# A two-layer Perceiver block: the state-space convolution as products of transforms, FiLM by token rows, norms by tile, and a new order in the top-32 attention

## The chip, the cores and the metric

The kernel runs on one NeuronCore of one Trainium2 chip, in fp32. The time is device microseconds of one execution. PE is the matrix engine (PEld its weight loads), DVE the vector engine, ACT the scalar engine, POOL GpSimd, SP the engine that issues most DMAs.

## The reference, cut to what matters

x is 8 batches of 64 tokens of 512 values, so 512 token rows, four tiles of 128. Six blocks follow one another, each `x = x + block(norm(x))`: cross attention to a context of 1601 rows, causal attention, experts, the block of this case, causal attention with rotary positions, experts with capacity.

```python
scores = where(mask, (x@Wq)(ctx@Wk)/sqrt(32)); keep top 32 per row; softmax; mean over 4 heads
c_t = (mean_weights @ (ctx@Wv)) * text_mask
x = layernorm(x_text, g_norm_in, b_norm_in)
scale_in, shift_in = split(c_t @ W_film_in + b_film_in)
x = x * (1 + gate * scale_in) + gate * shift_in
y = irfft(rfft(x, 2L) * rfft(K, 2L))[:L] + x * D_skip      # causal convolution, L = 64, per channel
y = y * (1 + gate * scale_out) + gate * shift_out
xt = x_text + y
xt = xt + gelu(layernorm(xt, g_ffn, b_ffn) @ W1 + b1) @ W2 + b2
out = layernorm(xt, g_norm_out, b_norm_out)
```

## The kernel before

Each block is one or two stages. A stage runs five engine programs side by side; at its end all engines meet in a barrier. Within a stage semaphores set the order, and the calls of each engine are written out by hand. Matmuls are fp32; each is two records in the trace.

**Context stage (d2), `xattn1_context`.** It loops over 8 batches. On PE `keys(b)` projects the context, `score(b)` makes two sets (r = 0, 1) of 128x1601 scores, `average(b)` averages the heads' weights into a transposed mean, `blend(b)` multiplies it with the context and turns the result. On DVE `pick(b, r)` takes the top 32 in four rounds of `max` and `match_replace`; after the second round of `pick(b, 0)` it runs `invert(b - 1)`, which waits for ACT's `exponentials(b - 1, 1)`. POOL subtracts, which gives the sparse weights. ACT runs `exponentials(b, r)`, copies keys, scores and means out of PSUM, and makes `share` from `invert`'s result; `average` waits for it. Before, ACT takes `put_keys(b + 2)` ahead of `exponentials(b, 1)` and PE takes `keys` and `score` ahead of `average`.

**FiLM and MLP stage (d3), `film_and_mlp`.** Channels lie on partitions. After the value product (L3165) the normed input is transposed (L3171); FiLM factors are made for four channel chunks (L3182) and copied out by ACT. The 64-tap convolution is shared: DVE takes chunks 0 and 1, a multiply-add per tap (L3055), POOL chunk 2 from taps scaled by ACT, PE chunk 3 with diagonal matrices (L3197). The result is transposed back (L3203), normed over all four tiles at once, transposed (L3208), scaled by DVE (L3088), and goes through W1 (L3216) and W2 (L3225, the last quarter of W2 lying in `w_out_film`). Then DVE adds, norms and adds x (L3098 to L3106).

**Next attention (e).** Its weights are loaded at its start (L1147, L1265). It norms x (`Norm.on_vector`, L138 to L146), and PE transposes (L1305) once all four tiles are normed; so do the other causal attention (b) and both expert stages (c, f).

## Time and profile before

| | us |
|---|---|
| median of 3 runs | 2467.47 (2466.85 to 2469.83) |
| the profiled execution | 2466.18 |
| span of its trace | 2464.5 |
| context stage | 1419 to 1741 |
| FiLM and MLP stage | 1741 to 2015 |
| next attention | 2017 to 2108 |

Starts are counted from the beginning of the span. An engine's row gives what it did, for how long, and in brackets how long it stood idle before and what ended that.

### The profile page before, as it was taken

Reading aid. Unit: us, or ns where it says so; the run is one execution under the profiler, and the core shown is the slowest. Engines: PE = TensorE matmul, PEld = TensorE weight load, DVE = VectorE, ACT = ScalarE, POOL = GpSimd, SP = SyncE. Lnnn points to the kernel's source line nnn. Section 1 sums busy time; section 2 is a strip of 40 time slices with the busy share of each in tenths; the row PEclk is TensorE's granted clock in tenths of the full one; section 3 lists DMA queues with packets and bytes.
Section 4 is the critical chain, followed back from the end, with each engine's and each line's share of the span. In section 5 each row is a group of like instructions: output and inputs, shape, how many; then the busy total and the mean of one; then the engine's idle time right before and its main releaser. Section 6 shows DMA issues by size and latency. Waiting matters only on the chain. (4 is left out here: it accounts for less than half of the span.)

```text
span 2464.5 us, 27034 instructions
## 1 busy us (share of the span) xinstructions
PE 2212.8 (90%) x10178; PEld 1333.9 (54%) x10178; DVE 1062.0 (43%) x2105; ACT 739.5 (30%) x1480; POOL 464.7 (19%) x535
## 2 busy tenths in 40 slices
PE   7989999999999986899999978887994968799999
PEld 3545555555555533444444435555452435699998
DVE  5465654655655124100000169778595034422120
ACT  2344444444544212211111143443280111111111
POOL 0000000000000010489986112112080000000010
PEclk9999999999999998899999986786896988899999
DMA  6102122122121321888887372431410010556662
GB/s 204 39 21 78 49 69 77 43 73 79 36 78 48 109 77 40 317 312 310 315 311 294 128 248 80 160 120 55 172 46 0 0 70 3 227 219 260 226 234 74
DMA packets 131282, 326.68 MB, mean 133 GB/s; under 512 B 39841, under 2 KB 89153, under 8 KB 111570
## 3 DMA queue, kind: packets, MB, share of 16 engines
q1 hardware_dynamic: 99440, 297.20, 33.6%
q10 hardware_dynamic: 29010, 19.16, 2.5%
q0 software_dynamic: 2704, 8.59, 1.0%
q8 instruction: 83, 1.36, 0.2%
q14 instruction: 45, 0.37, 0.0%
HBM read 302.89 MB, written 20.91 MB: 131 GB/s over the span
## 5 line engine op out<-in xcount | busy, mean ns | idle before, releaser
L874 PE MATMUL a_mix<-a_xn,a_probs_T 128*128 128x384 f32 (+1 forms) x832 | 313.1, 493 | 15.1 <-issue 10.2
L803 PE MATMUL a_sc<-a_wk_centred,a_ctx_T 128*128 128x512 f32 x624 | 288.3, 599 | 4.9 <-DVE a_wk_centred L552 2.6
L874 PEld LDWEIGHTS a_mix<-a_xn,a_probs_T 128*128 128x128 f32 (+1 forms) x832 | 145.8, 191 | 120.6 <-issue 73.0
L1830 PE MATMUL c_gate_up<-c_w_wide,c_h_rows 128*128 128x512 f32 x480 | 210.9, 592 | 0.0
L803 PEld LDWEIGHTS a_sc<-a_wk_centred,a_ctx_T 128*128 128x128 f32 x624 | 117.7, 192 | 129.4 <-issue 105.0
L1734 DVE TENSOR_TENSOR c_hidden<-c_silu,c_gate_up 128x512 f32<-128x512 f32 x38 | 26.1, 688 | 365.5 <-PE c_gate_up L1830 354.1
L1830 PEld LDWEIGHTS c_gate_up<-c_w_wide,c_h_rows 128*128 128x128 f32 x480 | 90.2, 190 | 108.0 <-issue 108.0
L2290 PE MATMUL f_ring<-f_picked_T,f_w 128*128 128x160 f32 x1024 | 143.5, 300 | 0.0
L2305 PE MATMUL f_ring<-f_hidden,f_w 128*128 128x160 f32 x1024 | 141.4, 300 | 0.4 <-ACT f_hidden L2179 0.4
L2290 PEld LDWEIGHTS f_ring<-f_picked_T,f_w 128*128 128x128 f32 x1024 | 139.9, 190 | 0.2
L2305 PEld LDWEIGHTS f_ring<-f_hidden,f_w 128*128 128x128 f32 x1024 | 139.3, 190 | 0.9 <-ACT f_hidden L2179 0.6
L1873 PE MATMUL c_y<-c_w_down,c_hidden_T 128*128 128x512 f32 x304 | 136.6, 593 | 0.0
L462 DVE SCALAR_TENSOR_TENSOR a_keys<-a_k_bias,a_std,a_sc 128x512 f32<-128x512 f32 (+1 forms) x104 | 77.1, 741 | 129.0 <-PE a_sc L803 129.0
L421 POOL TENSOR_SCALAR a_mask<-a_mask 128x896 bf16<-128x896 uint8 x8 | 7.5, 941 | 625.3 <-DVE a_top L491 607.1
L616 ACT ACTIVATE a_sq<-a_keys 128x512 f32<-128x512 f32 (+1 forms) x104 | 65.6, 630 | 196.2 <-DVE a_keys L462 196.2
L2841 PE MATMUL d_mean<-d_share,d_scores 128*128 128x64 f32 (+1 forms) x416 | 87.5, 414 | 21.8 <-ACT d_share L2747 9.1
L491 DVE CUSTOM_DVE_ANT_0 a_probs<-a_sc,a_mask 128x896 f32<-128x896 f32 x64 | 67.3, 1089 | 82.6 <-PE a_sc L834 82.6
L2841 PEld LDWEIGHTS d_mean<-d_share,d_scores 128*128 128x128 f32 (+1 forms) x416 | 86.0, 325 | 23.2 <-issue 12.9
L2647 POOL TENSOR_TENSOR d_scores<-d_scores,d_left 128x1601 f32<-128x1601 f32 x15 | 51.0, 3399 | 231.1 <-ACTq L2740 231.1
L3055 DVE SCALAR_TENSOR_TENSOR d_conv<-d_xin,kern,d_conv 128x504 f32<-128x504 f32 (+62 forms) x126 | 88.6, 703 | 4.6
L2663 DVE MAX8 d_best<-d_left 128x8 f32<-128x1601 f32 x48 | 87.6, 1826 | 1.4
L2667 DVE MATCH_REPLACE8 d_left<-d_best,d_left 128x1601 f32<-128x1601 f32 x48 | 86.9, 1811 | 0.0
(525 smaller groups left out, 3508.3 us busy)
## 6 DMA issues: line engine op xcount, KB each, us to landing
c_w_wide<-in_L_ffn_W SPq DMA_DIRECT2D x68, 1024.0 KB, 6.9
f_w<-in_L_ffn_W SPq DMA_DIRECT2D x32, 2048.0 KB, 8.5
c_w_down<-in_L_ffn_W SPq DMA_DIRECT2D x34, 1024.0 KB, 7.2
a_ctx_T<-in_ctx_T SPq DMA_DIRECT2D x48, 384.0 KB, 3.5
a_xn<-in_ctx SPq DMA_DIRECT2D x24, 768.0 KB, 7.1
d_context_T<-in_ctx_T SPq DMA_DIRECT2D x24, 768.0 KB, 10.7
d_context<-in_ctx SPq DMA_DIRECT2D x8, 2304.0 KB
mixed_context<-a_mixed_T ACTq DMA_DIRECT2D x84, 64.0 KB, 1.8
```

Source lines behind the costliest of these rows:

```text
L462: dve.scalar_tensor_tensor(out=keys[0:m, n % 4, :], in0=k_bias[0:m, :], scalar=std[0:m, t:t + 1], in1=key_bank(b, t)[0:m, :], op0=ALU.mult ...
L491: dve.tensor_tensor_reduce(out=probs[:, n % 2 * 2 + h, :].rearrange("p (c n) -> p c n", c=2), in0=sc[h][:, :, 0:BANK], in1=mask[:].rearran ...
L803: last = pe.matmul(key_bank(b, t), ctx_T[:, n % AHEAD, k, cols], wk_centred[:, k, :], start=(k == 0), stop=(k == KC - 1))
L874: ins = pe.matmul(mix[:, 0:DC], probs_T[0:m, t, p * P:(p + 1) * P], xn[0:m, b % 2, t, :], start=(t == 0), stop=(t == CT - 1))
L1830: last = pe.matmul(gate_up[2 * (u % 2) + part][:], h[:, k, :], w_wide[:, i % WIDE_RING, k, :], start=(k == 0), stop=(k == KD - 1))
L1873: last = pe.matmul(y[t % 2][:], hidden_T[:, u % 2, k, :], w_down[:, i % DOWN_RING, k, :], start=(c == 0 and k == 0), stop=(c == 1 and k == ...
L2290: last = pe.matmul(ring[use % 3][:, (m - lo) * CAP:(m - lo + 1) * CAP], w1[:, i % CHUNKS, k, at:at + P], picked_T[:, e % 2, k, :], start=( ...
L2305: last = pe.matmul(ring[use % 3][:, (m - lo) * CAP:(m - lo + 1) * CAP], w2[:, i % CHUNKS, k, at:at + P], hidden[:, k, :], start=(k == 0), ...
L2663: own.did(dve.max(eight, src))
L2667: ins = dve.match_replace(left[:, r, :], eight, src, MASKED)
L2841: last = pe.matmul(mean[t // 8][0:m, t % 8, :], scores[:, b % KEEP, r, t * P:t * P + m], share[:, r, :], start=(r == 0), stop=(r == 1))
L3055: own.did(dve.scalar_tensor_tensor(out=out[:, :, l:SEQ], in0=src[:, :, 0:SEQ - l], scalar=g.kern[:, k, l:l + 1], in1=out[:, :, l:SEQ], op0 ...
```

## The change

The convolution becomes products with constant matrices of cosines and sines (`waves`, a new input): with tokens on partitions, `transform(t)` takes two batches of a tile to 128 spectrum rows each, DVE multiplies by the kernel's spectrum (`multiply`), `transform_back(t)` sums two products back to 64 tokens per batch. FiLM factors come out by token rows and DVE applies them from PSUM. The norm before W1 runs tile by tile; ACT scales three turned tiles and DVE the last. The end of the block runs tile by tile and makes the next attention's norm as well; that attention's weights are loaded into W1's room once W1 is used up. In attention b and expert stages c and f, PE starts to transpose with the first normed tile (the hunk of b and e is shown; e has no norm left to wait for). In the context stage the order of ACT, PE and the loads changes. A stage `h` is put around d3 and e.

Of film_and_mlp the new lines are shown; what they replace stands above.

```diff
         def _(pe):
-            pe.wait_ge(norm.normed, NT)
             for t in range(NT):
+                if not normed:
+                    pe.wait_ge(norm.normed, t + 1)
                 for k in range(KD):
                     last = pe.transpose(ring[t][:, k, :], g.hn[:, t, k * P:(k + 1) * P], g.ident[:])
...
             load_turned(3)
+            load_turned(4)
             for b in range(2, NB):
                 load_context(b)
-                if b + 2 < NB:
-                    load_turned(b + 2)
+                if b + 3 < NB:
+                    load_turned(b + 3)
             early.load(sp, d)
...
             act.wait_ge(stack_ready, 2)
+            exponentials(0, 0)
+            put_keys(2)
             for b in range(NB):
-                exponentials(b, 0)
-                if b >= 1:
-                    put_mix(b - 1)
-                if b + 2 < NB:
+                exponentials(b, 1)
+                if 1 <= b and b + 2 < NB:
                     put_keys(b + 2)
-                exponentials(b, 1)
-                if b + 2 < NB:
-                    put_scores(b + 2)
                 if b < NB - 1:
                     put_shares(b)
                 put_mean(b)
+                if b < NB - 1:
+                    exponentials(b + 1, 0)
+                    put_mix(b)
+                if b + 2 < NB:
+                    put_scores(b + 2)
             put_mix(NB - 1)
...
             score(1)
+            keys(2)
             pe.wait_ge(stack_ready, 2)
             for b in range(NB):
-                if b + 2 < NB:
-                    keys(b + 2)
-                    score(b + 2)
                 average(b)
                 blend(b)
+                if b + 2 < NB:
+                    score(b + 2)
+                if b + 3 < NB:
+                    keys(b + 3)
...
+class Ahead:
+    def __init__(self, s):
+        self.room = s.sb("room", [P, KD * 2048])
+        self.w = self.room[:, 0:KD * 10 * P].rearrange("p (k n) -> p k n", k=KD)
+        self.wo = self.room[:, KD * 10 * P:KD * 14 * P].rearrange("p (k n) -> p k n", k=KD)
+        self.wv = self.room[:, KD * 14 * P:KD * 14 * P + KD * 32].rearrange("p (k n) -> p k n", k=KD)
+        self.qk_in, self.v_in, self.o_in = s.sem("qk_in"), s.sem("v_in"), s.sem("o_in")
+    def load(self, sp, d):
+        for h in (slice(0, KD // 2), slice(KD // 2, KD)):
+            sp.dma_start(self.w[:, h, :], d["L1_attn_qk"][:, h, :]).then_inc(self.qk_in, 16)
+        sp.dma_start(self.wv, d["L1_attn_wv"]).then_inc(self.v_in, 16)
+        sp.dma_start(self.wo, d["L1_attn_wo"]).then_inc(self.o_in, 16)
...
+            sp.wait_ge(ring_full, R_WIDE + FC)
+            ahead.load(sp, d)
...
+            norm.on_vector(dve, g.hn, xin)
+            gate = vecs["mod_gate"][:, 0:1]
+            def gated(t):
+                own.did(dve.tensor_scalar(t[:, 0:D], t[:, 0:D], gate, 1.0, ALU.mult, ALU.add))
+                own.did(dve.tensor_scalar(t[:, D:2 * D], t[:, D:2 * D], gate, None, ALU.mult))
+            gated(early_long["b_film_in"])
+            def each(out, left, right, op):
+                for t in range(NT):
+                    own.did(dve.tensor_tensor(out[:, t, :], left[:, t, :], right, op))
+                own.wait()
+            each(xin, xin, early_long["g_norm_in"][:], ALU.mult)
+            each(xin, xin, early_long["b_norm_in"][:], ALU.add)
+            each(rest, xin, early_long["b_film_in"][:, 0:D], ALU.mult)
+            each(rest, rest, early_long["b_film_in"][:, D:2 * D], ALU.add)
+            def modulate(t):
+                u = R_IN + 2 * t
+                dve.wait_ge(ring_full, u + 1)
+                own.did(dve.tensor_tensor(xin[:, t, :], xin[:, t, :], ring[u % 4][:], ALU.mult))
+                own.wait()
+                dve.tensor_tensor(rest[:, t, :], rest[:, t, :], xin[:, t, :], ALU.add).then_inc(film_out, 1)
+                dve.wait_ge(film_out, 2 * t + 1)
+                dve.wait_ge(ring_full, u + 2)
+                own.did(dve.tensor_tensor(xin[:, t, :], rest[:, t, :], ring[(u + 1) % 4][:], ALU.add))
+                own.wait()
+                dve.sem_inc(film_out, 1)
+                dve.sem_inc(modulated, 1)
+            def multiply(b):
+                dve.wait_ge(spectrum_full, b + 1)
+                dve.tensor_tensor(hidden[:, b, :], y[b % 4][:], kern_re[:], ALU.mult).then_inc(spectrum_out, 1)
+                dve.tensor_tensor(hidden[:, NB + b, :], y[b % 4][:], kern_im[:], ALU.mult).then_inc(spectrum_out, 1)
+            def finish(t):
+                u = R_OUT + 2 * t
+                dve.wait_ge(ring_full, u + 1)
+                dve.tensor_tensor(rest[:, t, :], b_film_out[:, 0:D], ring[u % 4][:], ALU.add
+                                  ).then_inc(film_out, 1)
+                dve.wait_ge(film_out, 2 * NT + 2 * t + 1)
+                dve.wait_ge(signal_full, t + 1)
+                own.did(dve.tensor_tensor(rest[:, t, :], rest[:, t, :], y[t][:], ALU.mult))
+                own.wait()
+                own.did(dve.tensor_tensor(rest[:, t, :], rest[:, t, :], xt[:, t, :], ALU.add))
+                own.wait()
+                dve.wait_ge(ring_full, u + 2)
+                own.did(dve.tensor_tensor(xt[:, t, :], rest[:, t, :], ring[(u + 1) % 4][:], ALU.add))
+                own.wait()
+                dve.sem_inc(film_out, 1)
+            def measure(i, t, src):
+                own.did(dve.bn_stats(end_stats[:, i, t, :], src))
+                own.wait()
+                dve.bn_aggr(end_mv[:, i, t, :], end_stats[:, i, t, :]).then_inc(end_measured, 1)
+            def normalize(i, t, src, dst, done=None):
+                dve.wait_ge(end_rooted, ROOTS.index((i, t)) + 1)
+                own.did(dve.reciprocal(end_rstd[:, i, t:t + 1], end_rstd[:, i, t:t + 1]))
+                own.wait()
+                ins = dve.tensor_scalar(dst, src, end_mv[:, i, t, 0:1], end_rstd[:, i, t:t + 1], ALU.subtract, ALU.mult)
+                if done is not None:
+                    ins.then_inc(done, 1)
+                else:
+                    own.did(ins)
+                    own.wait()
+            def add_hidden(t):
+                dve.wait_ge(y_full, t + 1)
+                own.did(dve.tensor_tensor(xt[:, t, :], xt[:, t, :], y[t][:], ALU.add))
+                own.wait()
+                measure(1, t, xt[:, t, :])
+            def end_tile(t):
+                normalize(1, t, xt[:, t, :], xt[:, t, :])
+                own.did(dve.tensor_tensor(xt[:, t, :], xt[:, t, :], long["g_norm_out"][:], ALU.mult))
+                own.wait()
+                own.did(dve.tensor_tensor(g.x[:, t, :], g.x[:, t, :], xt[:, t, :], ALU.add))
+                own.wait()
+                measure(2, t, g.x[:, t, :])
             for t in range(NT):
+                modulate(t)
+                if t == 0:
+                    dve.wait_ge(kern_out, 3)
                 else:
+                    multiply(2 * t - 2)
+                    multiply(2 * t - 1)
+            dve.wait_ge(b_out_in, 16)
+            gated(b_film_out)
             own.wait()
+            each(xt, g.hn, b_film_out[:, D:2 * D], ALU.add)
+            multiply(2 * NT - 2)
+            multiply(2 * NT - 1)
             for t in range(NT):
+                finish(t)
+                measure(0, t, xt[:, t, :])
+                if t:
+                    normalize(0, t - 1, xt[:, t - 1, :], g.hn[:, t - 1, :], mlp_normed)
+            normalize(0, NT - 1, xt[:, NT - 1, :], g.hn[:, NT - 1, :], mlp_normed)
             dve.wait_ge(long_in, 16 * len(long))
             for t in range(NT):
                 own.did(dve.tensor_tensor(xt[:, t, :], xt[:, t, :], long["b2"][:], ALU.add))
+            dve.wait_ge(turned_full, NT)
+            for k in range(KD):
+                last = dve.tensor_scalar(turned[:, k, (NT - 1) * P:NT * P], y[NT - 1][:, k * P:(k + 1) * P],
+                                         vecs["g_ffn"][:, k:k + 1], vecs["b_ffn"][:, k:k + 1], ALU.mult, ALU.add)
+            last.then_inc(scaled_by_dve, 1)
             for t in range(NT):
                 own.did(dve.tensor_tensor(g.x[:, t, :], g.x[:, t, :], long["b_norm_out"][:], ALU.add))
             own.wait()
+            for i in range(NT + 2):
+                if i < NT:
+                    add_hidden(i)
+                if 0 <= i - 1 < NT:
+                    end_tile(i - 1)
+                if 0 <= i - 2 < NT:
+                    normalize(2, i - 2, g.x[:, i - 2, :], g.hn[:, i - 2, :])
...
+            act.dma_start(waves[:], d["waves"]).then_inc(waves_in, 16)
+            act.dma_start(b_film_out[:], rows(d["L1_xattn_b_film_out"])).then_inc(b_out_in, 16)
+            act.wait_ge(kern_full, 1)
+            act.activation(kern_T[0:SEQ, :], y[0][0:SEQ, :], ACT.Copy).then_inc(kern_out, 1)
             norm.on_scalar(act, g.eps[:])
+            act.wait_ge(v_in, early.v_count)
             for m in range(KD):
                 act.wait_ge(ring_full, m + 1)
+                act.activation(value_T[:, m, :], ring[m % 4][:], ACT.Copy, scale=vecs["mod_gate"][:, 0:1]).then_inc(value_out, 1)
+                if m == 1:
+                    for i, t in enumerate((kern_re, kern_im)):
+                        act.wait_ge(kern_full, 2 + i)
+                        act.activation(t[:], y[1 + i][:], ACT.Copy).then_inc(kern_out, 1)
+            def root(n):
+                i, t = ROOTS[n]
+                act.wait_ge(end_measured, n + 1)
+                act.activation(end_rstd[:, i, t:t + 1], end_mv[:, i, t, 1:2], ACT.Sqrt, bias=g.eps[:]).then_inc(end_rooted, 1)
+            def scale(t):
+                act.wait_ge(turned_full, t + 1)
+                for k in range(KD):
+                    last = act.activation(turned[:, k, t * P:(t + 1) * P], y[t][:, k * P:(k + 1) * P], ACT.Identity,
+                                          bias=vecs["b_ffn"][:, k:k + 1], scale=vecs["g_ffn"][:, k:k + 1])
+                last.then_inc(scaled_by_act, 1)
+            root(0)
+            root(1)
+            root(2)
+            scale(0)
+            scale(1)
+            root(3)
+            scale(2)
             for m in range(FC):
                 u = R_WIDE + m
                 act.wait_ge(ring_full, u + 1)
                 act.activation(hidden[:, m, :], ring[u % 4][:], ACT.Gelu,
+                               bias=vecs["b1"][:, m:m + 1]).then_inc(wide_out, 1)
+            for n in range(NT, len(ROOTS)):
+                root(n)
...
+            for k in range(KD):
+                last = pe.transpose(y[0][0:SEQ, k * P:(k + 1) * P], g.kern[:, k, :], g.ident[:])
+            last.then_inc(kern_full, 1)
+            def values(m):
                 for k in range(KC):
                     last = pe.matmul(ring[m % 4][:], w_v[:, k, m * P:(m + 1) * P], c_T[:, k, :], start=(k == 0),
                                      stop=(k == KC - 1))
                 last.then_inc(ring_full, 1)
+            pe.wait_ge(w_v_in, 16)
+            pe.wait_ge(masked, KC)
+            values(0)
+            values(1)
+            pe.wait_ge(waves_in, 16)
+            pe.wait_ge(kern_out, 1)
+            for i, w in enumerate((taps_re, taps_im)):
+                pe.matmul(y[1 + i][:], w[0:SEQ, :], kern_T[0:SEQ, :], start=True, stop=True).then_inc(kern_full, 1)
+            values(2)
+            values(3)
+            pe.wait_ge(value_out, KD)
             pe.wait_ge(w_film_in, 32)
+            def film(t, outer):
                 w = w_out_film if outer else w_in_film
                 for j in range(2):
+                    n = (2 * NT if outer else 0) + 2 * t + j
+                    u = R_IN + n
+                    if n >= 4:
+                        pe.wait_ge(film_out, n - 3)
                     for i in range(KD):
+                        last = pe.matmul(ring[u % 4][:], value_T[:, i, t * P:(t + 1) * P], w[:, i, j * D:(j + 1) * D],
                                          start=(i == 0), stop=(i == KD - 1))
                     last.then_inc(ring_full, 1)
+            def transform(t):
+                pe.wait_ge(modulated, t + 1)
+                if t == 0:
+                    pe.wait_ge(kern_out, 3)
+                for b in (2 * t, 2 * t + 1):
+                    if b >= 4:
+                        pe.wait_ge(spectrum_out, 2 * (b - 4) + 2)
+                    half = slice(b % 2 * SEQ, (b % 2 + 1) * SEQ)
+                    pe.matmul(y[b % 4][:], forward[half, :], xin[half, t, :], start=True, stop=True
+                              ).then_inc(spectrum_full, 1)
+            def transform_back(t):
+                pe.wait_ge(spectrum_out, max(4 * t + 4, 2 * (t + 4) + 2))
+                for i, w in enumerate((back_re, back_im)):
+                    for h in range(2):
+                        last = pe.matmul(y[t][h * SEQ:(h + 1) * SEQ, :], w, hidden[:, i * NB + 2 * t + h, :],
+                                         start=(i == 0), stop=(i == 1), skip_group_check=True)
+                last.then_inc(signal_full, 1)
+            film(0, False)
+            film(1, False)
+            transform(0)
+            film(2, False)
+            transform(1)
+            film(3, False)
+            transform(2)
+            film(0, True)
+            transform(3)
+            film(1, True)
+            transform_back(0)
+            transform_back(1)
+            film(2, True)
+            transform_back(2)
+            transform_back(3)
+            film(3, True)
             for t in range(NT):
+                pe.wait_ge(mlp_normed, t + 1)
                 for k in range(KD):
                     last = pe.transpose(y[t][:, k * P:(k + 1) * P], g.hn[:, t, k * P:(k + 1) * P], g.ident[:])
                 last.then_inc(turned_full, 1)
+            pe.wait_ge(scaled_by_act, NT - 1)
+            pe.wait_ge(scaled_by_dve, 1)
...
+                    if q == 3:
+                        last.then_inc(y_full, 1)
...
+                with Stage(nc, "h") as s2:
+                    ahead = Ahead(s2)
+                    film_and_mlp(g, early, ahead)
+                    causal_attention(g, "e", "L1_attn_qk", 1, True, "L1_attn_wv", 32, "L1_attn_wo", None,
+                                     1.0 / float(np.sqrt(32.0)), ahead)
```

## Rows read from the trace of the kernel before

**Rows 1.** The page: busy tenths of PE in 40 slices, and two costly groups (busy us, mean ns).

```profile
PE   7989999999999986899999978887994968799999
...
L2663 DVE MAX8 d_best<-d_left 128x8 f32<-128x1601 f32 x48 | 87.6, 1826 | 1.4
L2667 DVE MATCH_REPLACE8 d_left<-d_best,d_left 128x1601 f32<-128x1601 f32 x48 | 86.9, 1811 | 0.0
```

**Rows 2.** Windows: stretch, span, busy us (x count) by engine, granted PE clock, DMA share, GB/s.

```profile
1488.00:1492.00 4.00, 4.00 (x21) 4.00 (x21) 3.93 (x5) 0.32 (x1) 0.00 (x0) 0.50 0.00 0
1756.00:1784.00 28.00, 28.00 (x72) 12.82 (x71) 23.22 (x42) 5.44 (x7) 3.13 (x2) 1.00 0.41 159
```

**Rows 3.** Timeline of PE, FiLM and MLP stage: start us, duration us, [idle before].

```profile
1743.09 11.97 PE L3165 MATMUL d_ring<-d_c_T,d_w_v 128*128 128x512 f32 x24 [3.43 <-DVE d_c_T L3021]
...
1756.64 27.63 PE L3182 MATMUL d_ring<-d_value_T,d_w_in_film 128*128 128x512 f32 x64
...
1870.70 3.67 PE L3203 MATMUL d_y<-ident,d_conv 128*128 128x128 f32 x16 [26.50 <-DVE d_conv L3066]
...
1887.05 58.02 PE L3216 MATMUL d_ring<-d_xin,d_w_wide 128*128 128x512 f32 x128 [2.80 <-DVE d_xin L3088]
...
1986.10 13.90 PE L3225 MATMUL d_y<-d_w_out_film,d_hidden 128*128 128x512 f32 x32
```

**Rows 4.** Timeline of DVE, the same stage.

```profile
1826.79 36.85 DVE L3055 SCALAR_TENSOR_TENSOR d_conv<-d_xin,kern,d_conv 128x504 f32<-128x504 f32 x63
...
1864.40 0.69 DVE L3043 TENSOR_TENSOR d_conv<-d_conv,d_hidden 128x512 f32<-128x512 f32 x1
...
1881.80 5.19 DVE L3088 TENSOR_SCALAR d_xin<-d_y,d_v_g_ffn,d_v_b_ffn 128x128 f32<-128x128 f32 x16 [1.28 <-PE d_y L3208]
1886.90 2.49 DVE L3094 TENSOR_TENSOR d_xt<-d_xt,d_r_b 128x512 f32<-128x512 f32 x4
```

**Rows 5.** Waits of DVE, context stage: us in total, times, longest.

```profile
DVE d_total L2678 <- ACTq L2740: 30.2, 5, 7.3
```

**Rows 6.** Timeline of DVE, context stage: `invert` of the first and seventh batch.

```profile
1482.59 0.17 DVE L2678 RECIPROCAL d_total<-d_total 128x2 f32<-128x2 f32 x1
...
1693.53 0.17 DVE L2678 RECIPROCAL d_total<-d_total 128x2 f32<-128x2 f32 x1
```

**Rows 7.** Timeline of PE, context stage: one round and two `score` calls.

```profile
1452.91 1.13 PE L2818 MATMUL d_ks<-d_k_T,d_q_diag 64*128 64x512 f32 x4
...
1484.55 10.95 PE L2841 MATMUL d_mean<-d_share,d_scores 128*128 128x64 f32 x52 [1.49 <-ACT d_share L2747]
1495.42 7.09 PE L2857 MATMUL d_mix<-d_context,d_mean_T 128*64 128x384 f32 x26
1503.09 0.88 PE L2864 MATMUL d_turned<-d_stack,d_mixed 128*128 128x64 f32 x6 [0.58 <-ACT d_mixed L2763]
1503.81 8.56 PE L2807 MATMUL d_ks<-d_context_T,d_wk 128*128 128x512 f32 x24
...
1517.62 2.08 PE L2818 MATMUL d_ks<-d_k_T,d_q_diag 64*128 64x512 f32 x4 [2.90 <-ACT d_scores L2717]
```

**Rows 8.** Timeline of ACT, context stage.

```profile
1456.91 1.32 ACT L2717 ACTIVATE d_scores<-d_ks 128x512 f32<-128x512 f32 x4 [0.45 <-PE d_ks L2822]
...
1483.89 0.60 ACT L2747 ACTIVATE d_share<-d_quarter,d_total 128x64 f32<-128x64 f32 x2
```

**Rows 9.** Timeline of DVE, end of the MLP and start of the next stage.

```profile
2012.97 2.50 DVE L3106 TENSOR_TENSOR x<-x,hn 128x512 f32<-128x512 f32 x4
2016.78 2.47 DVE L138 BATCH_NORM_STATS2 e_norm_stats<-x 128x6 f32<-128x512 f32 x4 [1.32 <-PEq L90]
...
2020.25 1.91 DVE L146 TENSOR_SCALAR hn<-x,e_norm_mv,e_norm_rstd 128x512 f32<-128x512 f32 x4
```

**Rows 10.** Timeline of PE at that start.

```profile
2022.22 2.19 PE L1305 MATMUL e_ring<-ident,hn 128*128 128x128 f32 x9 [22.22 <-DVE hn L146]
```

**Rows 11.** DMA issues, 1740 to 1770 us: KB each, us to landing.

```profile
d_w_out_film<-in_L_xattn_W_film_out SPq DMA_DIRECT2D x1, 2048.0 KB, 12.4
```

289 lines of the change are left out of this document (73 added, 216 removed).

## The prediction

> **What bounds the kernel now.** I read the page first. PE is nine tenths busy in most slices, with dips in the second half [rows 1], so time is to be had where PE waits, and those places lie in the two stages that the change rewrites. The waits, the timelines of PE and DVE and a table of windows then say what bounds each place.
>
> *Context stage.* Between the reciprocals of the first and the seventh batch lie 210.9 us, 35.2 a round [rows 6]. DVE's only wait there is 30.2 us in five pieces, for the exponentials of r = 1 [rows 5]: `invert` stands in the middle of `pick`, and ACT, its releaser, first copies keys that PE is still making. Without that wait a batch would take (210.9 - 30.2) / 6 = 30.1 us of DVE, 3.8 for each of its eight pairs of `max` and `match_replace` (1.83 and 1.81 busy) [rows 1].
>
> *FiLM and convolution.* PE makes 64 film records from 1756.64 on in 27.5 us, 0.43 each at the full clock, and as many again for the second matrix, to 1811.6 [rows 2, 3]. Then DVE sets the pace: its second chunk alone is 36.9 us of taps [rows 4], and PE stands idle for 26.5 us before it can turn the result [rows 3]. W1 starts at 1887.05.
>
> *After the MLP.* The last W2 record ends at 2000.0 [rows 3], DVE adds and norms until 2015.5 (2012.97 + 2.50), then come two barriers, and one more norm of four tiles; PE turns its first tile at 2022.22 after 22.2 us of idleness [rows 9, 10].
>
> **The change part by part.** The sum is made against the profiled execution, 2466.18 us; the median of the runs is 1.3 above it, and the forecast for the median is moved by as much. The smallest change that this kernel's measurement can tell is about 0.2%, 5 us.
>
> *1. Context order.* ACT now takes `exponentials(b, 1)` first, so DVE's wait of 30.2 goes. What is late next is the scores. `score(b + 2)` moves behind `average(b)` and `blend(b)`, and `average` needs `share`, which needs `invert`, 7.6 us into `pick(b + 1, 0)`. The loop from one start of a pick to the next is then: two pairs 7.6, the reciprocal 0.2 [rows 6], `share` 0.6 [rows 8]; `average` 10.9 (1484.55 to 1495.42); `blend`, the copy and the turn 8.4 (to 1503.81) [rows 7]; `score` and its copies, 1452.91 to 1458.23 less the last copy, 5.0 [rows 7, 8]. That is 32.7, above DVE's 30.1. PE's own work in it is 10.9 + 8.4 + 8.6 (`keys`) + 4.1 = 32.0, so it is nearly full. The reason for a little less: `average` ran at half clock [rows 2], 0.21 a record, behind a wait of 1.5; now only some 0.7 us of idleness come ahead of it. At the pace of the turning records, 0.88 / 6 = 0.147, it would take 7.6. I take 32.3: 6 x (35.2 - 32.3) = 17 gained. Bounds: DVE's pace of 30.1 gives 30; `score` with two of four pieces at half clock, 2.08 for 1.13 as at 1517.62 [rows 7], adds 2 a round and leaves 3. POOL's subtraction runs beside DVE's pairs as before; the load of `keys(b + 3)` is issued a round ahead, behind one `blend`.
>
> *2. Convolution.* Removed: 126 taps of DVE, 63 of POOL, 128 diagonal records, two sets of transposes. PE's chain, from the same start (values end at 1755.0 [rows 3]): two products for the kernel's spectrum, four records, 1.7; the last value copy, by the copy ahead of the turn (0.58 for 384 columns [rows 7]), 0.7; so films start at 1757.4. Films: 16 x 8 records x 0.43 = 55.0. `transform`: four tiles, each two products on different row halves like `score`'s four records in 1.13 [rows 7], 4.3 together. `transform_back`: 8 records a tile on column halves like `blend`. There 26 records of 384 columns took 7.09, 0.27 each, partly at half clock; 1.9 a tile at full clock, 7.6 together. Were the halves not to overlap, it would be 8 x 0.43 = 3.4 a tile and 1.7 for a `transform`: 6 and 2.5 more. Film work ends at 1757.4 + 55.0 + 4.3 + 7.6 = 1824.3.
>
> DVE stays under that. Its 16 row operations before the first tile cost 0.62 each (L3094's 2.49 / 4) [rows 4], and end near 1760, when the first film bank (1757.4 + 3.4) is full; four banks are a cover of 6.9 us, after which each us late is one of PE. A tile then needs 3 operations of 0.73 to modulate (0.69 and a step) and 4 to multiply, 5 us against PE's 6.9; at the end 4 more and the norm, beside 6.9 of film again.
>
> Behind the film work: PE turns tiles 0 and 1 (3.67 / 4 = 0.92 each [rows 3]). ACT's order is `scale(0)`, `scale(1)`, and only then the last root; each `scale` costs four operations, by DVE's 5.19 / 16 = 0.32 some 1.3. So the root comes at 1824.3 + 0.9 + 2.6 = 1827.8, with it and DVE's two small steps the last tile is normed at 1828.8. Queued on DVE ahead of its own scaling are the four additions of b2, 2.5; they hide the transpose of tile 3. Scaling 1.3 and a crossing: W1 starts at 1832.8, 54.3 earlier. Bounds: 57 with transposes at full clock and a shorter end, 45.5 with no overlap of halves. Loads: `w_out_film` landed 12.4 us after an issue half a microsecond into the stage, near 1753.8, as the last of 4 MB [rows 11]. The 0.77 MB that ACT now issues beside them cost 2.3 at that rate: 1756.1, before 1757.4. Were `waves` to land only then, PE would stand 6 us before the kernel's products.
>
> One rule speaks against many small products between the films. PE takes `blend` on 64 columns at 1495.42, before `average`'s last record on 128 ends [rows 7], so I see no gap. 
>
> *4. End of the block.* Tiles of W2 come 3.4 us apart, the last at 2000.0 on the old axis. DVE per tile, with a step of 0.11 after each dependent operation: add 0.73, measure 0.85; two factors and an addition 3.0 with the second measure; the next norm 0.7. That is 5.3, above 3.4, so DVE sets the end: first two tiles to 1997.7, then 5.3, 5.3 and 4.4, 2012.7. The pieces are from 2.47 / 4 and 1.91 / 4 [rows 9] and rows 4. One barrier, half of the 1.3 between 2015.47 and 2016.78 [rows 9]: PE turns its first tile at 2013.4 instead of 2022.2, 8.8 gained. The next attention's weights, loaded beside W2, have 55 us for 3.7 MB; without that they would now be waited for. Bounds: 6, if every root's crossing shows, to 11, if the steps vanish.
>
> *5. Stage `h`* adds barriers at the end of attention e, two times 0.65: 1.3 lost.
>
> *6. Transposes with the first tile* in b, c and f: three tiles of 1.91 / 4 = 0.48 [rows 9], 1.4 each, 4.3 gained; at 0.92 a tile PE stays behind DVE, so all of it passes on. If the work behind waits for loads it is 1.
>
> Sum: -17 - 54.3 - 8.8 + 1.3 - 4.3 = -83. 2466.2 - 83 = 2383, and 2384 for the median.
>
> **The rivals.**
> - *The new order gains nothing.* PE's 32.0 of work a round leaves no slack; a little more half clock in `score` makes it the old 35. For it: `score` at 1517.62 at half clock behind an idle 2.9. Against: `keys` and `score` now follow `blend` without a pause. 17 less 3 lost: 2398.
> - *DVE's pace.* `average` runs at full clock, a round is 30.1: 13 more, 2371. Against it: the `average` of rows 2 stood at 0.50.
> - *Stalls in the film stage*, from halves that don't overlap or `waves` late: 8 to 14 more, 2392 to 2398.
> - *Slower.* PE, denser now, is held at 1.2 GHz. Film work is 72 us at full clock and the MLP 113; each would double. It decides from 83 us of such work on: the film stage alone gives 2456, both 2569. Against it: the granted clock was 1.00 in a stretch without a gap [rows 2].
>
> **How the numbers follow.** Forecast 0.58, its own range 2374 to 2394; order without gain 0.14; DVE's pace 0.12; stalls 0.13; slower 0.02; within 0.2% 0.01. All bounds at once give 102 and 54 less, 2366 and 2414. From 2368 to 2404 the range takes in all cases but the ends of two and the last two, at most 2 in 10. Faster 0.97, same 0.01, slower 0.02.
>
> **What would show it.** Reciprocals of `invert` 32 to 33 us apart, and DVE's wait now for scores; W1 starting 92 us after the value product's stage begins, with PE without a gap over 1 us from the first film to the last; the last normed tile waiting for a root behind `scale(1)`; some 13 us from the last W2 record to the first transpose of the next attention. Wrong would make it: PE idle between films (loads, or DVE behind), clock under 1.0 in the film stage, rounds of 35, or weights of the next attention waited for.

## The result and the profile after

| | before | after |
|---|---|---|
| median | 2467.16 us (2465.91 to 2469.83, 4 runs) | 2385.72 us (2384.64 to 2387.93, 4 runs) |
| span of the trace | 2464.5 | 2384.3 |
| mean granted clock of PE | 0.931 | 0.947 |

The ratio is 0.967, with an interval of 0.9653 to 0.9686. The change takes 81.4 us, where 83 were forecast. The stages show how well that sum was made (each from its start to the next one's; us). They are read from the two profiled executions, and add up to 80.2 less:

| stretch | before | after | difference | forecast |
|---|---|---|---|---|
| first stage (a) | 884.2 | 884.9 | +0.7 | 0 |
| attention b | 94.9 | 95.6 | +0.7 | -1.4 |
| experts c | 440.2 | 440.0 | -0.2 | -1.4 |
| context stage | 321.7 | 295.1 | -26.6 | -17 |
| FiLM stage, to the first W1 record | 146.0 | 94.1 | -51.9 | -54.3 |
| W1 and W2 | 113.0 | 112.9 | -0.1 | 0 |
| last W2 record to the next attention's first transpose | 22.2 | 14.1 | -8.2 | -8.8 |
| from there to stage f | 86.9 | 91.8 | +4.9 | +1.3 |
| experts f | 355.4 | 355.9 | +0.5 | -1.4 |

So the total is right partly by luck: the context stage gave 9.6 more than forecast, and the other stretches 12.4 less together.

**Context stage.** Timeline of DVE, the reciprocal of `invert` in the first and the seventh batch; it answers to [rows 6]:

```profile
1483.70 0.17 DVE L2692 RECIPROCAL d_total<-d_total 128x2 f32<-128x2 f32 x1
...
1668.96 0.17 DVE L2692 RECIPROCAL d_total<-d_total 128x2 f32<-128x2 f32 x1
```

Six rounds take 185.3, 30.9 each, and not 32.3; they alternate between 31.5 to 31.8 and 30.1. The waits of DVE in this stage, which answer to [rows 5], have no wait for an exponential any more:

```profile
DVE d_best L2677 <- ACT d_scores L2731: 24.5, 4, 20.1
```

Of these 24.5 us, 20.1 are the first scores, at the start. The other 4.4, three waits of about 1.5, are what makes every second round longer than 30.1: there DVE waits for scores, as the prediction had it for all rounds. Timeline of PE, the first three calls of `average` (52 records) and one of `blend` (26), which answer to [rows 7]:

```profile
1484.58 10.91 PE L2857 MATMUL d_mean<-d_share,d_scores 128*128 128x64 f32 x52 [17.25 <-ACT d_share L2761]
...
1516.82 5.81 PE L2857 MATMUL d_mean<-d_share,d_scores 128*128 128x64 f32 x52 [0.79 <-ACT d_share L2761]
1522.56 4.73 PE L2873 MATMUL d_mix<-d_context,d_mean_T 128*64 128x384 f32 x26
...
1546.47 10.94 PE L2857 MATMUL d_mean<-d_share,d_scores 128*128 128x64 f32 x52 [4.41 <-ACT d_share L2761]
```

The same 52 records take 10.9 or 5.8 us in turn: behind an idle stretch of 0.79 they are quick, behind one of 4.41 slow. The windows, of the first and the second `average`, say at which clock; the column behind the last busy time is the granted one:

```profile
1488.00:1492.00 4.00, 4.00 (x21) 4.00 (x21) 3.97 (x4) 0.32 (x1) 0.00 (x0) 0.50 0.00 0
1517.00:1521.00 4.00, 4.00 (x38) 4.00 (x38) 3.93 (x4) 0.36 (x1) 0.00 (x0) 1.00 0.88 291
```

**FiLM stage.** Timeline of PE from the stage's start to W1, which answers to [rows 3]:

```profile
1717.66 8.08 PE L3213 MATMUL d_ring<-d_c_T,d_w_v 128*128 128x512 f32 x12 [1.44 <-DVE d_c_T L3041]
1725.68 1.98 PE L3224 MATMUL d_y<-d_kern_T,d_waves 64*128 64x512 f32 x4
1727.59 5.42 PE L3213 MATMUL d_ring<-d_c_T,d_w_v 128*128 128x512 f32 x12
1733.78 14.00 PE L3239 MATMUL d_ring<-d_w_in_film,d_value_T 128*128 128x512 f32 x32 [0.78 <-ACT d_value_T L3172]
1747.71 1.13 PE L3251 MATMUL d_y<-d_xin,d_waves 64*128 64x512 f32 x4
1748.77 7.13 PE L3239 MATMUL d_ring<-d_w_in_film,d_value_T 128*128 128x512 f32 x16
...
1780.21 3.65 PE L3259 MATMUL d_y<-d_hidden,d_waves 128*64 128x512 f32 x16
...
1794.44 7.13 PE L3239 MATMUL d_ring<-d_w_out_film,d_value_T 128*128 128x512 f32 x16
1801.41 1.04 PE L3282 MATMUL d_y<-ident,hn 128*128 128x128 f32 x8
1804.11 0.66 PE L3282 MATMUL d_y<-ident,hn 128*128 128x128 f32 x4 [1.66 <-DVE hn L3104]
1805.96 1.11 PE L3282 MATMUL d_y<-ident,hn 128*128 128x128 f32 x4 [1.20 <-DVE hn L3104]
1809.70 57.93 PE L3294 MATMUL d_ring<-d_xin,h_room 128*128 128x512 f32 x128 [2.62 <-issue]
```

From the first film to 1801.5 PE has no gap: 67.7 us, forecast 66.9. A transform takes its 1.13, two of `transform_back` 3.65. The stage itself starts at 1715.62 with the kernel's transposes, which are not shown. Behind the films come three short idle stretches up to W1. ACT and DVE in those, from their timelines:

```profile
1802.05 2.90 ACT L3186 ACTIVATE d_xin<-d_y,d_v_b_ffn,d_v_g_ffn 128x128 f32<-128x128 f32 x8 [5.62 <-PE d_y L3282]
1804.81 0.33 ACT L3181 ACTIVATE d_end_rstd<-d_end_mv,eps 128x1 f32<-128x1 f32 x1
```

```profile
1805.16 0.16 DVE L3102 RECIPROCAL d_end_rstd<-d_end_rstd 128x1 f32<-128x1 f32 x1 [1.11 <-ACT d_end_rstd L3181]
...
1805.83 2.49 DVE L3145 TENSOR_TENSOR d_xt<-d_xt,d_r_b 128x512 f32<-128x512 f32 x4
1808.24 1.36 DVE L3148 TENSOR_SCALAR d_xin<-d_y,d_v_g_ffn,d_v_b_ffn 128x128 f32<-128x128 f32 x4
```

The last root stands behind both scalings, and DVE's own scaling behind the additions of b2, as forecast.

**End of the block and attention e.** Timeline of PE, which answers to [rows 10]:

```profile
1936.62 3.65 PE L1318 MATMUL e_ring<-ident,hn 128*128 128x128 f32 x16 [14.06 <-PEq L90]
1941.04 36.51 PE L1327 MATMUL e_ring<-hT,h_room 128*128 128x512 f32 x80 [0.78 <-ACT hT L1282]
```

In the kernel before, the same 80 records took 34.57. That loss is what some of the later experiments are about.

### The profile page after: what moved, and what is told of

It is laid out like the page before. It is cut to its first block and busy times, and to the rows that moved or that the text cites. A ratio compares the mean times of both kernels' runs of the same rounds, so it can differ in the third digit from the quotient of the medians.

```text
span 2384.3 us, 26510 instructions
## 1 busy us (share of the span) xinstructions
PE 2169.0 (91%) x10074; PEld 1293.6 (54%) x10074; DVE 995.8 (42%) x2002; ACT 691.1 (29%) x1360; POOL 408.3 (17%) x467
## 5 line engine op out<-in xcount | busy, mean ns | idle before, releaser
L1747 DVE TENSOR_TENSOR c_hidden<-c_silu,c_gate_up 128x512 f32<-128x512 f32 x38 | 26.1, 688 | 364.2 <-PE c_gate_up L1843 354.2
L2857 PE MATMUL d_mean<-d_share,d_scores 128*128 128x64 f32 (+1 forms) x416 | 72.1, 361 | 48.6 <-ACT d_share L2761 42.0
L2857 PEld LDWEIGHTS d_mean<-d_share,d_scores 128*128 128x128 f32 (+1 forms) x416 | 70.8, 273 | 49.6 <-ACT d_share L2761 25.6
L2681 DVE MATCH_REPLACE8 d_left<-d_best,d_left 128x1601 f32<-128x1601 f32 x48 | 86.9, 1811 | 0.0
L1886 PEld LDWEIGHTS c_y<-c_w_down,c_hidden_T 128*128 128x128 f32 x304 | 54.9, 190 | 55.0 <-issue 55.0
```

The lines of the kernel that those rows point to most:

```text
L1886: last = pe.matmul(y[t % 2][:], hidden_T[:, u % 2, k, :], w_down[:, i % DOWN_RING, k, :], start=(c == 0 and k == 0), stop=(c == 1 and k == ...
L2681: ins = dve.match_replace(left[:, r, :], eight, src, MASKED)
L2857: last = pe.matmul(mean[t // 8][0:m, t % 8, :], scores[:, b % KEEP, r, t * P:t * P + m], share[:, r, :], start=(r == 0), stop=(r == 1))
```

## The experiments

Each batch of four ran on one chip beside the kernel before, whose medians there were 2469.27, 2469.94 and 2469.08. Stages are compared by their own lengths, in one profiled execution each, since the first one alone differs by up to 4 us from run to run. The changed kernel itself had a median of 2385.72 us at first and of 2388.32 in the last batch, so a difference of 3 us between medians of different batches says nothing.

**First batch: the parts of the change by themselves.** *order_alone* is the kernel before with the new context stage, *old_order* the changed kernel with the old one; the edit is the context part of the diff above, put in or taken out whole.

> The kernel before with only the context stage's new order of ACT, PE and loads. Theory A (the trace of after): where only 0.8 us of PE idleness precede it, the average of the heads runs at full clock in 5.8 us instead of 10.9, so rounds alternate between 30.1 and 31.6 us, and the stage is 26 to 27 us shorter: about 2441 for a median before of 2467. Rival B (the sum on record): every round is near 32.3, 17 us gained: 2450. Rival C: the gain of the stage comes from its other neighbours in the change, and alone the order gives under 5.

> The changed kernel with the context stage as before. By theory A the time rises by 26 to 27 us, to about 2412, with rounds of 35 and every average at 10.9 us. By B it rises by 17. The rest of the change is then worth 55 us alone.

Measured: 2444.28 us, ratio 0.9903 (0.9888 to 0.9917), and 2411.26 us, ratio 0.9762 (0.9748 to 0.9776). By the medians the order is worth 25.0 us alone and 25.5 in the changed kernel; the context stage itself is 26.3 shorter in the one (321.7 to 295.5) and 27.2 in the other (322.3 to 295.1). So it depends on nothing else in the change. Its slow and quick averages alternate here too; two rows of PE in *order_alone*:

```profile
1518.67 5.81 PE L2844 MATMUL d_mean<-d_share,d_scores 128*128 128x64 f32 x52 [0.79 <-ACT d_share L2748]
1548.32 10.95 PE L2844 MATMUL d_mean<-d_share,d_scores 128*128 128x64 f32 x52 [4.41 <-ACT d_share L2748]
```

In *old_order* DVE waits for the exponentials again, and every average is slow, the first six behind an idle stretch of 1.5 to 1.7, the last two behind longer ones:

```profile
DVE d_total L2691 <- ACTq L2753: 31.4, 5, 7.5
```

```profile
1521.98 10.94 PE L2854 MATMUL d_mean<-d_share,d_scores 128*128 128x64 f32 x52 [1.50 <-ACT d_share L2760]
```

*heads_alone* is the kernel before with the transposes from the first tile in all four stages:

```diff
-            pe.wait_ge(norm.normed, NT)
             for t in range(NT):
+                pe.wait_ge(norm.normed, t + 1)
```

> The kernel before with only the transposes of the four stage heads started per tile. As forecast, each head is 1.4 us earlier and it passes on: 5 to 6 us less, 2461. Theory D (the trace of after): PE starts earlier, but the granted clock rises no earlier, so the first products run longer at 1.2 GHz; the gain is under 1.5 us in all, 2466 to 2468.

Measured: 2470.4 us, ratio 1.0003 (0.9993 to 1.0014), so the 5 to 6 us of the forecast are not there. All transposes do start 1.4 earlier after their norm. What follows differs from stage to stage. In b the 64 products start 1.1 earlier and are no longer than before, 27.70; the timeline of PE in this kernel:

```profile
895.26 27.70 PE L1314 MATMUL b_ring<-hT,b_w 128*128 128x512 f32 x64 [0.78 <-ACT hT L1270]
```

Of these 1.1, 0.7 is lost near the end of the stage, where transposes between the heads take 1.96 in place of 1.09 us; b is 0.4 shorter. In the changed kernel, with the same code for b, the products are longer, and a window at their start (granted clock third from the end) shows why:

```profile
893.40 29.52 PE L1327 MATMUL b_ring<-hT,b_w 128*128 128x512 f32 x64 [0.78 <-ACT hT L1282]
```

```profile
893.00:897.00 4.00, 3.60 (x5) 1.56 (x6) 0.00 (x0) 3.45 (x10) 0.00 (x0) 0.50 1.00 340
```

Nor do the old heads always have them quick: in *order_alone*, whose b is that of the kernel before, they took 29.83. Over all runs b took 93.6 to 95.7 with the new heads, 94.9 and 97.3 with the old ones, so a single profile can't price the edit there. In c the routing product, 32 records, gets longer by more than the start was moved, first before, then *heads_alone*:

```profile
988.90 4.55 PE L1812 MATMUL c_y<-c_w_route,hT 128*128 128x8 f32 x32 [0.69 <-ACT hT L1761]
```

```profile
989.73 6.99 PE L1812 MATMUL c_y<-c_w_route,hT 128*128 128x8 f32 x32 [0.69 <-ACT hT L1761]
```

Behind it the wait for a load shrinks from 3.01 to 1.68, and c is as long as before. In e the 80 products wait for their weights and then take 36.26 for 34.57:

```profile
2028.08 36.26 PE L1314 MATMUL e_ring<-hT,e_w 128*128 128x512 f32 x80 [1.39 <-DMA e_w<-in_L_attn_qk]
```

The output product of e took 16.97 for 14.00, and from the last W2 record to stage f this kernel needs 4.5 more than the kernel before. That is more than b, c and f gained together; stage f is 0.7 shorter.

*late_weights* is the changed kernel with attention e's weights loaded at its own start.

> The changed kernel with the next attention's weights loaded at its own start again, as before the change. The first product would start 4.4 us after the stage's start, and the halves landed 8.4 and 9.0 us after issue before: 4 to 5 us slower, 2390. Rival: the clock is at 1.2 GHz then anyway and a later start falls into a faster clock, so 2 to 3 us only; or 0, if the load is hidden.

Measured: 2388.63 us, ratio 0.9676 (0.9664 to 0.9689). In its trace the products wait:

```profile
1946.96 37.50 PE L1326 MATMUL e_ring<-hT,h_room 128*128 128x512 f32 x80 [5.65 <-DMA h_room<-in_L_attn_qk]
```

They start 4.9 later than in the changed kernel. Stage f starts 95.8 after the first transpose and not 91.8: loading ahead is worth 4.0 by stages, since the output product happened to be 1.4 shorter here. By the medians it is 2.9, which is less than this measurement can tell.

**Second batch: queues, clock and tiles.** *root_first*:

```diff
             scale(0)
-            scale(1)
             root(3)
+            scale(1)
             scale(2)
...
-            dve.wait_ge(long_in, 16 * len(long))
-            for t in range(NT):
-                own.did(dve.tensor_tensor(xt[:, t, :], xt[:, t, :], long["b2"][:], ALU.add))
...
             last.then_inc(scaled_by_dve, 1)
+            dve.wait_ge(long_in, 16 * len(long))
+            for t in range(NT):
+                own.did(dve.tensor_tensor(xt[:, t, :], xt[:, t, :], long["b2"][:], ALU.add))
```

> The changed kernel with two moves behind the film work: ACT takes the last root ahead of scale(1), and DVE's four additions of b2 come behind its scaling of tile 3. In the changed kernel W1 starts 8.2 us after the last film record (1801.5 to 1809.7); ACT's scale(0) and scale(1) took 2.90 together and the last reciprocal waited 1.11 for the root. My theory, that the queues of ACT and DVE are on the path there: the root comes about 1.1 earlier (it can't come before the last measure, 0.35 before scale(1) ends at the soonest), the additions' 2.5 were only partly covered by the transposes of tile 3, so W1 starts 1.5 to 2.5 earlier, about 0.08% of the run, 2384 us. Rival: DVE's scaling waits for the transposes of tile 3 anyway, so moving the additions gives nothing and the move of the root its 1.1 at most; if PE's last transposes at half clock set the start of W1, 0 to 0.5.

Measured: 2376.86 us, ratio 0.9619 (0.9606 to 0.9632), 9 less than the changed kernel by the medians, 11 by the stages from the films on, and far more than expected. PE behind the film work:

```profile
1804.50 1.04 PE L3282 MATMUL d_y<-ident,hn 128*128 128x128 f32 x8
1807.20 1.31 PE L3282 MATMUL d_y<-ident,hn 128*128 128x128 f32 x8 [1.66 <-DVE hn L3104]
1810.02 55.17 PE L3294 MATMUL d_ring<-d_xin,h_room 128*128 128x512 f32 x128 [1.51 <-ACT d_xin L3186]
```

W1 starts 5.52 after the start of these transposes and not 8.29, 2.8 less: the queues were on the path. W1's records take 55.17 and not 57.93, 2.8 less by the clock. Attention e is 3.9 shorter (87.8 from its first transpose to stage f, for 91.8) and stage f 1.6, also by the clock; that these two come from the edit is not shown, since in *busy_before_w1* below W1 is as quick and e takes 92.2 all the same. Windows of 2 us around the last transposes, first of the changed kernel, then of *root_first*:

```profile
1803.40:1805.40 2.00, 0.66 (x4) 0.42 (x4) 0.81 (x5) 2.00 (x8) 0.00 (x0) 0.90 0.98 410
1805.40:1807.40 2.00, 1.11 (x4) 0.71 (x4) 2.00 (x4) 1.98 (x5) 0.00 (x0) 0.50 0.09 37
```

```profile
1806.50:1808.50 2.00, 1.30 (x8) 0.84 (x8) 1.22 (x5) 2.00 (x8) 0.00 (x0) 1.00 0.97 397
1808.50:1810.50 2.00, 0.49 (x2) 0.30 (x2) 1.95 (x6) 1.98 (x5) 0.00 (x0) 1.00 0.11 45
```

*busy_context* keeps PE busy ahead of each average:

```diff
+            def busy(n):
+                for i in range(n):
+                    pe.matmul(mix[:], wk[:, 0, :], g.hT[:, 0, 0:DC], start=True, stop=True)
             for b in range(NB):
+                busy({0: 25, NB - 2: 20, NB - 1: 20}.get(b, 6))
                 average(b)
```

> The changed kernel with products that nobody reads, 128x384 each, written into the bank of mix ahead of every average: 25 ahead of the first (16 us; PE was idle for 17.25), 6 ahead of the second to the sixth (3.8 us; idle 0.8 or 4.4), 20 ahead of the last two (12.8 us; idle 13.6 and 6.6). Theory: only the granted clock makes average take 10.9 in place of 5.8 us, and PE's idleness ahead of it brings that clock down. Then all eight averages take 5.8, the rounds of invert are all at DVE's pace of 30.1 (six rounds 180.6 in place of 185.3), the last average and what follows it are 5 to 7 shorter, the context stage is 10 to 12 us shorter and the run 2374 to 2376. Rival 1: average's length comes from what runs beside it (DVE's pairs, ACT's reads, the loads), then the products change nothing or, where they are longer than the idleness, cost up to 3 us a round. Rival 2: the clock is right but DVE sets the pace of all rounds and the alternation is no loss: then only the end gains, 5 us.

Measured: 2380.73 us, ratio 0.9641 (0.9624 to 0.9658). The context stage takes 286.3 in place of 295.1, 8.8 less, but the median is only 5.0 less, and the profiled execution 2.7: in it attention e's output product (below) took 1.6 more, stage f 3.6, and the stages ahead of the edit 1.9. PE in the first two rounds (L2910 are the added products):

```profile
1469.16 16.34 PE L2910 MATMUL d_mix<-hT,d_wk 128*128 128x384 f32 x50
1486.52 5.81 PE L2857 MATMUL d_mean<-d_share,d_scores 128*128 128x64 f32 x52 [1.01 <-ACT d_share L2761]
...
1511.64 4.09 PE L2910 MATMUL d_mix<-hT,d_wk 128*128 128x384 f32 x12
1516.62 5.81 PE L2857 MATMUL d_mean<-d_share,d_scores 128*128 128x64 f32 x52 [0.90 <-ACT d_share L2761]
```

Seven of eight averages are quick, and the reciprocals lie 30.2 apart, (1666.7 - 1485.7) / 6. The same data, reads and loads run beside them, so it is the clock that made them slow, and without it DVE sets the pace. The sixth took 8.46: behind only 0.79 of idleness the clock fell while it ran, so short idleness ahead of the records does not always keep the clock up.

*busy_before_e* puts 15 products of 128x512 behind the last W2 record:

```diff
                     if q == 3:
                         last.then_inc(y_full, 1)
+            for i in range(15):
+                pe.matmul(ring[0][:], hidden[:, 0, 0:P], w_down[3][:, 0, :], start=True, stop=True)
```

> The changed kernel with 15 products of 128x512 that nobody reads behind the last W2 record, 12.8 us on PE, which was idle for 14.06 before the next attention's first transpose. From that transpose to the next stage's norm the changed kernel takes 91.8 us, the kernel before 86.9; I put 1.9 of it on the first products at a granted clock of 0.50 until 1945, 2.0 on the output product at the end of the attention, also partly at 0.50, and 1.0 on the barriers of stage h. Theory: with PE busy to the barrier the first 80 product records take 34.6 in place of 36.5 and the 16 transposes less than 3.65, 2 to 3 us gained, 2383; the output product, behind another idle stretch, stays at 16. Rival: the start of the attention is slow for its weights or for a longer way from hn to PE, then nothing changes.

Measured: 2382.95 us, ratio 0.9652 (0.9638 to 0.9665). PE at the start of e:

```profile
1936.69 1.95 PE L1318 MATMUL e_ring<-ident,hn 128*128 128x128 f32 x16 [1.19 <-PEq L90]
1939.57 34.57 PE L1327 MATMUL e_ring<-hT,h_room 128*128 128x512 f32 x80 [0.94 <-ACT hT L1282]
```

The first transpose stands where it stood, the transposes take 1.95 for 3.65, the products 34.57 for 36.51, and f starts 87.5 later, not 91.8. Of these 4.3, 2.9 lie ahead of the output product and 1.4 in it, 14.0 for 15.4, which I had said would stay. By the medians it is 2.8, by itself inside the noise; the stage is what shows it. But how much of the 4.3 the added products gave is open: *root_first* and *late_end* add none behind W2 and had the 34.57 and the 14.0 too. Only the quick transposes, 1.5 us with the earlier start of the products, are found in no kernel without them.

*late_end* adds one wait for all four tiles ahead of the end of the block:

```diff
+            dve.wait_ge(y_full, NT)
             for i in range(NT + 2):
```

> The changed kernel with one more wait: DVE starts the end of the block (add, norm, factors, next norm) only when all four tiles of W2 are done, so the tiles no longer overlap the last products of W2; all else is as changed. In the changed kernel DVE's first addition came at 1912.37, the last W2 record ended at 1922.56, and DVE ended at 1935.47 with 1.7 us of waiting in between. Theory, that DVE's queue sets the end and the tiles' overlap is the whole of the 8.2 us gained there: DVE starts at 1922.7, needs 21.4, and ends at 1944, 8.5 later; the run takes 2394. Rival: making the next norm inside the block, with one barrier and one set of waits less, is what gave the gain; then the loss is 4 at most, as in the kernel before, where four tiles together needed 13 from the last record and not 21.

Measured: 2388.01 us, ratio 0.967 (0.9656 to 0.9683). The chain behaves as the theory says. DVE ends at 1944.8, and PE follows:

```profile
1945.99 3.55 PE L1318 MATMUL e_ring<-ident,hn 128*128 128x128 f32 x16 [22.50 <-PEq L90]
```

22.5 us of idleness in place of 14.06: the overlap with W2's last tiles is worth 8.4, all of the 8.2 gained. Without it the new end is no better than the old one, 22.2, so the rest of the new end, one barrier less and the norm made by tile, comes to nothing together. The run lost 2.3 and not 8.4, because the products of e came at full clock, 34.57, its output product took 14.0 (together 4.6 less for e), and stage f 353.1 in place of 355.9.

**Third batch: control and sum.** *after_again* is the changed kernel once more.

> The changed kernel once more, unaltered, on the same chip as the three that follow: their times are read against this one. Both theories: 2384 to 2387 us; what its stages differ by from the first profile of it tells how far a single profile can be read (I expect 1 to 2 us, from loads in the first stage).

Measured: 2388.32 us (2383.93 to 2389.76), ratio 0.9668 (0.9652 to 0.9684). All its stages but the first are within 0.2 of the first profile, with half clock at the same places; the first is 2.0 longer.

*no_h* takes three semaphores from the outer stage, so that `h` ends without a barrier:

```diff
-        self.qk_in, self.v_in, self.o_in = s.sem("qk_in"), s.sem("v_in"), s.sem("o_in")
+        self.qk_in, self.v_in, self.o_in = outer.sem("ahead_qk_in"), outer.sem("ahead_v_in"), outer.sem("ahead_o_in")
...
-                    ahead = Ahead(s2)
+                    ahead = Ahead(s2, s)
```

> The changed kernel with the three semaphores of the next attention's loads taken from stage d, so that stage h only holds room and ends without clearing semaphores and without a barrier of its own. Theory: the way from the last output product of attention e to the first norm of stage f, 2.64 us in the changed kernel and 1.62 in the one before, is 1.6 again, the run 1.0 shorter. Rival: the records of that product end later for the granted clock and the barrier's share is nothing; or a microsecond earlier puts stage f on another phase of the clock, whose first 40 us were seen to differ by 2 to 3, and the sum is then anything from 3 less to 2 more.

Measured: 2386.33 us, ratio 0.9666 (0.9651 to 0.9681), no difference by the run. The 1.0 of the theory did not come: from the first transpose to stage f it is 91.4 for 91.8. From the end of DVE's last addition to f's norm it is 1.52, in the changed kernel 1.90, in the one before 0.89:

```profile
2027.21 2.47 DVE L138 BATCH_NORM_STATS2 f_norm_stats<-x 128x6 f32<-128x512 f32 x4 [1.52 <-PEq L90]
```

The barrier of stage h costs 0.4, not 0.65. The other 0.6 fits the end of stage d, which by the code came ahead of e before and now comes behind it; no run takes it away by itself.

*busy_before_w1*:

```diff
+            pe.wait_ge(film_out, 4 * NT - 3)
+            for i in range(3):
+                pe.matmul(ring[0][:], w_out_film[:, 2, 0:P], w_out_film[:, 2, 0:D], start=True, stop=True)
             pe.wait_ge(scaled_by_act, NT - 1)
```

> The changed kernel with three products of 128x512 that nobody reads between the last transposes and W1, 2.5 us in PE's wait of 2.62. The queues of ACT and DVE stay as they are, so W1 starts as before, at 94.1 us after the start of its stage. Theory: in the run with the root first, W1's 128 records took 55.2 in place of 57.9 because the idleness ahead of them fell from 2.6 to 1.5 and the granted clock stayed up, not because of the order of operands; then here too 55.2, 2.8 less, the run 2382 to 2383. Rival: W1's first records are slow because they wait for the turned tiles or for the first Gelu of ACT with its table load; then 57.9 stays and the run is no shorter.

Measured: 2385.82 us, ratio 0.9663 (0.9648 to 0.9678), 2.5 below *after_again* on the same chip, but the intervals overlap: no gain that can be told. Its rows say why:

```profile
1805.75 5.22 PE L3286 MATMUL d_ring<-d_w_out_film 128*128 128x512 f32 x6
1810.81 55.10 PE L3297 MATMUL d_ring<-d_xin,h_room 128*128 128x512 f32 x128
```

W1 takes 55.1 as the theory has it, and full speed from its first record rules out the turned tiles and the Gelu. But the added products fell into the half clock themselves, 0.87 a record, W1 started 2.2 late, and so they paid what W1 had paid. By the changed kernel's windows above the clock falls at about 1805, within the second of the two idle stretches, 1.66 and 1.20, that part the transposes. *root_first* removes the second, and there the clock stays up; that this is the reason is what is left, and no run shows it by itself.

*all_four* holds *root_first*, *busy_context*, *busy_before_e* and *no_h*.

> The edits together: the last root first and b2's additions later, products that nobody reads ahead of the averages and behind the last W2 record, and stage h without a barrier. By stages: context 8.8 shorter (295.1 to 286.3), W1's start 2.8 earlier and its records 2.8 shorter, attention e 4.3 shorter, barrier 1.0: 19.7 together, 2366 us. Theory that these are separate places: 2363 to 2370, the spread from the first 40 us of stage f at a clock of 0.66 to 0.74. Rival: the clock's falls and rises shift with all that comes before, so that the last two gains don't add up: 2370 to 2376.

Measured: 2369.78 us (2366.58 to 2374.76), ratio 0.9603 (0.9586 to 0.9621), 18.5 less than *after_again* by the medians and 16 by the ratios. Against that kernel: context 286.4 for 295.2 (-8.8), to W1 90.6 for 94.1 (-3.5), W1 and W2 110.1 for 112.9 (-2.8), e 86.5 for 91.8 (-5.2), f 357.5 for 356.0 (+1.5), the first stages 0.1 longer. The median lies at the edge between theory and rival; it is the stages that say the gains add up, and stage f takes 1.5 back. It is faster than both kernels.

## Why the prediction was right, and where it was not

**Context order.** The mechanism was right: DVE's wait of 30.2 went, and nothing else in the change is needed for it. The size was 9.6 too small, and the term that was mis-sized is `average`. The chain of 32.7 holds it at 10.9, half clock, and I took only 0.4 off, though the 7.6 worked out beside it would have made the chain 29.4, under DVE's 30.1. It measured 10.9 in one round and 5.81 in the next. With 10.9 the chain is what sets the round, 31.6. With 5.8, and `blend` at 4.7, it is well under DVE's 30.1, so DVE sets the pace, PE stands idle for 4.4, and the next average is at half clock again. The average over the two kinds of rounds is 30.9. My value for a record, 0.147, came from the six turning records of 128x64, whose 0.88 runs to the end of the last one and so is no pace; 52 records at full clock show 0.112. From the two levels of the clock, 10.9 / 2 = 5.5 was at hand. The rival "DVE's pace" was the nearer one in this stage, and in the changed kernel every average ran at the one level or the other, none at a mixture. So both mechanisms hold by turns, and a single pace for all rounds was wrong.

**Convolution.** The sum of the records was right to 0.8 us over 67.7, with no stall, and DVE under it. Films started 18.2 after the stage's start and not 16.4: twelve value records took 8.08, where twelve took 5.42 a little later. Together that is 13.5, where all 24 had taken 12.0 in the kernel before ([rows 3]), so a longer stretch at half clock behind the barrier (granted 0.50 until 7.5 us after the stage's start, before until 4.9) cost 1.5 of the 1.8 that were missing. Behind the film work W1 started 8.2 later (forecast 8.5), by the very queue that the prediction named. Of the 2.4 that are missing, 1.8 lie in the first step and 0.8 in the film work, and 0.3 came back behind it.

The halves overlap as in `blend`: 1.8 a tile. On the rule of the Trainium skill (TensorEngine Tiling, section "Key Properties", that a change of mode drains the engine): a film call of 16 records starts 7.07 before what follows it (1748.77 to 1755.84), where 16 records of an unbroken row take 6.87 (64 in 27.5, [rows 3]). That is 0.2 each, 1.2 for the six calls with another mode behind them, within the estimate of 1 to 2; the last film call, with transposes of its own mode behind it, took 6.97 (1794.44 to 1801.41). By that rule, the trace agrees; what else a waiting call might cost isn't told apart from it, since no kernel here had the waits without the change of mode.

**MLP.** Nothing, as forecast. It could have been worth 2.8: *root_first* shows that the half clock at its start can be avoided.

**Block end.** 8.2 for 8.8, and *late_end* shows that it is the overlap of tiles alone. DVE's 4.6 to 5.3 a tile set the end, as worked out; DVE ended 12.9 behind the last W2 record (forecast 12.7), and the way from there to the first transpose took 1.15, not 0.7.

**Stage h and attention e.** Forecast +1.3, measured +4.9. The barrier term was right to 0.3 (1.0). What was missing is the clock: 1.9 in the 80 products, 1.4 in the output product and 0.5 between them. *busy_before_e* is 4.3 shorter again, of which 1.5 are seen only with products added ahead of e.

**Transposes with the first tile.** Forecast -4.3, measured +1.0 over the three stages, and nothing in *heads_alone*. "All of it passes on" is the step that failed. The start that was won is given back in records at half clock (the routing product of c, e's products and output product, in b the transposes near the end or, in the changed kernel, the products), and in e a wait for the weights takes a part. Between kernels with the same code for b its products take 27.7 or 29.4 to 29.6, so what the edit costs or gains in a stage depends on more than the edit.

So the places where PE is dense came out as summed. The large misses are of one kind, the granted clock behind idleness, in both directions; the small ones are the barrier, 0.3, and the film work, 0.8.

## What to carry to other kernels

Where PE waits and then works, price the work at each of the clock's two levels and look at the idleness ahead of it, before and after the change; a start that is moved by a microsecond can be worth nothing if records behind it fall into the lower level. Removing a short wait on the way to a long run of products can be worth more than its own length: 2.8 us of waiting in *root_first* gave 2.8 more in W1's records. And read such changes by stages: medians of this kernel hide 3 us, and one stage's clock can cover another's gain.
